# Own moments by SBUF-to-SBUF transfers into free rows: 32 moment slots per tile in place of 36

## What is computed

```python
e = stack([tbl_f[ids[:, f]] for f in range(26)], axis=1)            # (2048, 26, 32)
x1 = einsum('bik,bjk,hij->bhk', e,  e, W1) + b1                      # 128 maps
x2 = einsum('bik,bjk,hij->bhk', x1, e, W2) + b2                      # 128 maps
z = sum(concat([x1, x2], axis=1), axis=-1)                           # (2048, 256)
h = relu(concat([z, dense_ctx], axis=1) @ W_top1 + b_top1)           # 512
h = relu(h @ W_top2 + b_top2)                                        # 256
y = h @ W_top3
```

## Time and profile before

| | us |
|---|---|
| median of 3 runs | 604.69 |
| lowest and highest | 596.48, 609.61 |
| the profiled execution's own time | 604.4 |
| span of its profile | 602.6 |
| mean granted TensorE clock in it | 0.952 of full |

### The profile page before, as it was taken

One profiled execution on the slowest core, in us unless ns is written; L12 is line 12 of the kernel. 1 busy time (PEld: TensorE's weight loads), 2 busy tenths in 40 slices (PEclk: granted clock), 3 DMA queues, 4 the chain that ended last, 5 costly groups with the idle time before them and its releaser, 6 DMA issues.

```text
span 602.6 us, 13628 instructions
## 1 busy us (share of the span) xinstructions
PE 523.6 (87%) x5314; PEld 498.1 (83%) x5314; DVE 454.4 (75%) x1253; ACT 256.9 (43%) x528; POOL 373.7 (62%) x275
## 2 busy tenths in 40 slices
PE   4846986975979989898889898988999789999997
PEld 4524975965979989898889898988989689999987
DVE  6626965949777979697787969595959697996762
ACT  6513762543433535253535262433435253535501
POOL 5774687258735868677676878685858765740100
PEclk9966997996979999998999999998999899999999
DMA  6640022021312141303030213222231303000000
GB/s 194 160 62 8 5 29 36 7 48 22 41 27 33 17 47 16 46 11 47 9 46 12 40 20 36 24 30 29 23 36 16 43 9 44 11 9 1 2 1 2
DMA packets 30925, 19.58 MB, mean 32 GB/s; under 512 B 5171, under 2 KB 30326, under 8 KB 30761
## 3 DMA queue, kind: packets, MB, share of 16 engines
q0 software_dynamic: 8512, 4.38, 10.7%
q1 hardware_dynamic: 22377, 14.73, 9.9%
HBM read 19.08 MB, written 0.01 MB: 32 GB/s over the span
## 4 chain that ended last, share of the span: by engine, by line
PE 83%; issue 7%; ACT 3%; DVE 3%; another core or an unknown queue 2%; DMA 1%; SPq 0%; ACTq 0%; DVEq 0%
PE psum L858 34%; PE psum L878 19%; PE psum L895 11%; PE psum L938 4%; PE psum L916 4%; PE psum L872 3%; PE psum L811 3%; ACT v L699 2%; PE psum L834 1%; PE psum L832 1%; DVE work L624 1%; DMA t_area<-in_L_rec_W 1%; PE psum L804 1%; PE psum L828 1%
## 5 line engine op out<-in xcount | busy, mean ns | idle before, releaser
L377 POOL DMA_INDIRECT emb<-in_tbl,idx x266 | 371.0, 1395 | 162.8 <-issue 76.4
L858 PE MATMUL psum<-diag,work 128*109 128x108 f32 x2048 | 222.2, 266 | 22.2 <-issue 9.1
L858 PEld LDWEIGHTS psum<-diag,work 128*109 128x109 f32 x2048 | 210.6, 180 | 29.2 <-issue 14.7
L728 ACT COPY t_area<-psum 109x432 f32<-109x432 f32 x256 | 130.4, 519 | 193.1 <-PE psum L858 177.4
L624 DVE TENSOR_TENSOR work<-embT 128x32 f32<-128x32 f32 (+12 forms) x416 | 129.2, 387 | 0.0
L895 PE MATMUL psum<-table_parts,onehot 125*128 125x96 bf16 x1350 | 72.7, 213 | 22.5 <-issue 12.4
L895 PEld LDWEIGHTS psum<-table_parts,onehot 125*128 125x128 bf16 x1350 | 66.2, 102 | 27.8 <-issue 22.9
L878 PE MATMUL psum<-t_area,v 128*128 128x128 f32 x608 | 73.0, 277 | 5.3 <-issue 5.3
L878 PEld LDWEIGHTS psum<-t_area,v 128*128 128x128 f32 x608 | 70.5, 193 | 6.4 <-issue 6.3
L712 ACT COPY diag<-embT 32x416 f32<-32x416 f32 x128 | 69.9, 546 | 10.4 <-DVE embT L608 8.8
L454 DVE TENSOR_SCALAR onehot<-ids_left 125x1280 bf16<-125x1280 bf16 (+1 forms) x150 | 57.3, 453 | 0.5
(11 more groups left out here) (103 smaller groups left out, 467.6 us busy)
## 6 DMA issues: line engine op xcount, KB each, us to landing
ids_all<-in_short_ids SPq DMA_DIRECT2D x15, 625.0 KB
emb<-in_tbl,idx POOLq DMA_INDIRECT x266
t_area<-in_L_rec_W SPq DMA_DIRECT2D x1, 1664.0 KB
work<-in_W_top SPq DMA_DIRECT2D x2, 512.0 KB
onehot<-in_tbl SPq DMA_DIRECT2D x5, 156.2 KB
onehot<-in_tbl SPq DMA_DIRECT2D x5, 125.0 KB
t_area<-in_L_rec_W SPq DMA_DIRECT2D x1, 338.0 KB, 3.2
idx<-in_ids SPq DMA_DIRECT2D x4, 52.0 KB, 1.9
```

Source lines behind the costliest of these rows:

```text
L377: eng.indirect_dma_start(emb[n][:, f * K:(f + 1) * K], None, tables[f], bass.IndirectOffsetOnAxis(ap=idx[:, t * F + f:t * F + f + 1], axis=0),
L728: nc.scalar.copy(dst, src).then_inc(t_out, 1)
L858: last = nc.tensor.matmul(dst[:, :, c * TS:(c + 1) * TS], pairs[:, half, g % HALF, c, :], diag[:, g, :, :], start=True, stop=True)
```

## The change

The 13 own slots of a group, as far as their rows are wanted, are cut into six pieces. SyncE copies each from `tsum` to rows 92 and up of the other slots in `tsum` by a DMA, which makes 12 transfers a tile with 284 rows of 512 to 3072 bytes; the other slots then have up to 128 rows for `cin`. Two own slots a group (5 and 6) and the single-field moments ("cross") don't fit; ScalarE copies them: 10 small copies a tile, six of one slot and four of three, three, three and two slots, of 13 to 28 partitions. These `loose` slots are double-buffered. `cin` has 5 + 27 = 32 matmuls. `pack` on VectorE is gone with its buffers and the memsets of `last_packs`.

v is laid out alike: own parts are drained into `staged` and moved by 6 transfers a group. `make_v` has 18 jobs (5 first-layer matmuls where 15 stood), `v_out` 36 copies. VectorE's split of W_top1 and W_top2 moves from behind both halves of `extra` to between them.

```diff
+GAP = CONST + 1
+DEEP = NP - GAP
+PIECES = [(7, 0, DEEP, 0, 0, 6), (11, DEEP, 2 * DEEP, 6, 0, 2), (8, DEEP, tri(11), 8, 0, 3), (0, 0, tri(3), 8, tri(11) - DEEP, 3),
+          (11, 2 * DEEP, CONST, 11, 0, 2), (3, 0, tri(5), 11, CONST - 2 * DEEP, 2)]
+LOOSE = (5, 6)
+CROSS = [(0, 3), (2, 5), (5, 8), (8, 11), (11, 13)]
...
 @block.sync
-            for t in range(2, TILES):
-                eng.wait_ge(left_ready, t - 1)
-                load_ids_all(t)
+            for c in range(2):
+                eng.wait_ge(prep_out, AFTER_V1 if c else AFTER_MOVED + JOBS_W1 + JOBS_OWN)
+                for mu, lo, hi, slot, at, count in PIECES:
+                    dst = V_OTHER + HF * c + slot
+                    eng.dma_start(v[GAP + at:GAP + at + hi - lo, dst:dst + count, :],
+                                  staged[c][lo:hi, mu:mu + count, :]).then_inc(v_moved[c], 16)
+            def pack(t):
+                n = t % 2
+                eng.wait_ge(t_out, UNITS * (t + 1))
+                for mu, lo, hi, slot, at, count in PIECES:
+                    for c in range(2):
+                        src, dst = c * TS + c * HF + mu, c * TS + (1 - c) * HF + slot
+                        eng.dma_start(tsum[GAP + at:GAP + at + hi - lo, n, dst:dst + count, :],
+                                      tsum[lo:hi, n, src:src + count, :]).then_inc(packed[n], 16)
+            for t in range(1, TILES + 1):
+                if t + 1 < TILES:
+                    eng.wait_ge(left_ready, t)
+                    load_ids_all(t + 1)
+                pack(t - 1)
...
 @block.vector
+            for c in range(2):
+                nc.vector.tensor_copy(first_layer[:, c, 0:GAP - c], w1p[:, c, 0:GAP - c])
...
-            nc.vector.memset(packs[:, :, :], 0.0).then_inc(dve_own, 1)
...
+            nc.vector.memset(spare[:, :, :], 0.0).then_inc(loose_zero, 1)
...
-                if not known or t >= 2:
-                    pack(t - 1, 1 - n)
...
 @block.scalar
+            def loose_out(t, n):
+                into = loose[:, n]
+                eng.wait_ge(t_out, UNITS * t + UNITS)
+                for j, (lo, hi) in enumerate(CROSS):
+                    src = tsum[FIELD0:ROWS, n, TS + HF + lo:TS + HF + hi, :]
+                    if j == 0:
+                        for c in range(2):
+                            nc.scalar.copy(tsum[FIELD0:ROWS, n, c * TS + ONE, :], src[:, c, :])
+                    else:
+                        nc.scalar.copy(into[K * (j - 1):K * (j - 1) + HF, 0:hi - lo, :], src)
+                for c in range(2):
+                    for a, mu in enumerate(LOOSE):
+                        at, rows = K * (len(LOOSE) * c + a), tri(mu + 1)
+                        last = nc.scalar.copy(into[at:at + rows, CROSSES, :], tsum[0:rows, n, c * TS + c * HF + mu, :])
+                last.then_inc(loose_ready, 1)
...
                 if u == 0 and isinstance(t, int) and t == 0:
                     eng.wait_ge(extra_ready, 2)
+                    eng.wait_ge(v_moved[0], 16 * len(PIECES))
                 if u == 0 and not (isinstance(t, int) and t < 2):
                     eng.wait_ge(z_full, t - 1)
-                    eng.wait_ge(packs_ready, t - 1)
...
+                if not known or 1 <= t < TILES:
+                    loose_out(t, n)
...
 @block.tensor
-            def cin(t, n):
-                moments, packed = tsum[:, n], last_packs if isinstance(t, int) and t == TILES - 1 else packs
-                eng.wait_ge(packs_ready, t + 1)
+            def cin(t, i, n):
+                eng.wait_ge(packed[n], 16 * PACK_MOVES * (i + 1))
...
+                eng.wait_ge(loose_ready, t + 1)
+                terms = [(V_ONE + c, tsum[:, n, c * TS + ONE, :], ROWS) for c in range(2)]
+                terms += [(V_CROSS + s, loose[:, n, s, :], NP) for s in range(CROSSES)]
...
+                terms = [(V_OTHER + HF * c + nu, tsum[:, n, c * TS + (1 - c) * HF + nu, :], ROWS_OF[nu])
+                         for c in range(2) for nu in range(HF)] + [(V_LOOSE, loose[:, n, CROSSES, :], NP)]
```

More of the change, by code:

```diff
@@ L282, in build @@
         w2T_jobs = [range(m, min(m + 4, F)) for m in range(0, F, 4)]
[L283 to L287, removed]
+        v_jobs = [([("first", 0, s, NP) for s in range(4)], [(0, 4, 0, NP, v[:, 0:4, :])]),
+                  ([("first", 0, 4, NP)], [(0, 1, 0, NP, v[:, 4:5, :])])]
@@ L288, in build, with other_jobs @@
         JOBS_W1 = len(v_jobs)
-        for c in range(2):
+        def other_jobs(c):
+            jobs = []
             for lo in range(0, HF, 4):
                 hi = min(lo + 4, HF)
-                at = (32 * 2 * c, V_P28 + lo) if lo < N28 else (32 * (2 * c + 1), V_P28 + NU_LAST)
-                v_jobs.append(([("other", c, nu, CONST + 1) for nu in range(lo, hi)],
-                               [(0, hi - lo, 0, LOW, LOW * c, V_OTHER + lo), (0, hi - lo, LOW, CONST + 1, *at)]))
+                slot = V_OTHER + HF * c + lo
+                jobs.append(([("other", c, nu, GAP) for nu in range(lo, hi)], [(0, hi - lo, 0, GAP, v[:, slot:slot + hi - lo, :])]))
+            return jobs
@@ L295, in build, with own_jobs @@
+        def own_jobs(c):
+            jobs = []
             for lo in range(0, HF, 4):
+                mus = range(lo, min(lo + 4, HF))
                 moves = []
-                for mu in range(lo, min(lo + 4, HF)):
+                for mu in mus:
                     rows = tri(mu + 1)
[L299 to L304, removed]
@@ L305, in build @@
-                v_jobs.append(([("own", c, mu, tri(mu + 1)) for mu in range(lo, min(lo + 4, HF))], moves))
+                    if mu in LOOSE:
+                        at = K * (len(LOOSE) * c + LOOSE.index(mu))
+                        moves.append((mu - lo, 1, 0, rows, v[at:at + rows, V_LOOSE:V_LOOSE + 1, :]))
+                    else:
+                        moves.append((mu - lo, 1, 0, rows, staged[c][0:rows, mu:mu + 1, :]))
+                jobs.append(([("own", c, mu, tri(mu + 1)) for mu in mus], moves))
@@ L824, in make_v @@
                         dst = prep_bank(n)[0:rows, a * H:(a + 1) * H]
-                        if what == "one":
-                            last = nc.tensor.matmul(dst, w1p[:, c, 0:rows], ident[:, :], start=True, stop=True)
-                        elif what == "cross":
-                            last = nc.tensor.matmul(dst, w1s[c][:, HF + third, 0:rows], ident[:, :], start=True, stop=True)
+                        if what == "first":
+                            last = nc.tensor.matmul(dst, first_layer[:, third, :], ident[:, :], start=True, stop=True)
                         else:
@@ L964, in _ @@
                 short_rows(1, part)
-            cin(0, 0)
+            cin(0, 0, 0)
             for t in range(1, 4):
```

167 lines of the change are left out of this document (69 added, 98 removed).

## The result

| | before | after |
|---|---|---|
| median, us | 602.77 (4 runs) | 648.66 (4 runs) |
| lowest and highest | 596.48, 609.61 | 645.38, 657.79 |
| profiled execution, span | 602.6 | 646.5 |
| mean granted TensorE clock | 0.952 | 0.897 |

What follows compares the result with a forecast made beforehand. TensorE was taken as the bound, by its number of instructions and its standstill. From 604.4 us, 14.3 for `cin` and 4.5 for the preparation gave 585.6, taken as 585.5; range 555 to 603.

Steps and rivals of the forecast that it cites:

- `cin` loses 14.3 us: TensorE's `cin`: four matmuls of 36 fewer in each of 16 tiles, all on the path; -14.3 us, bounds -14.3 and -10.
- VectorE's packing, 0 us; below zero at best: Packing, 8.5 us a tile, leaves VectorE; TensorE never waited for it, so 0, or -35 if it causes the pauses.
- and the change leaves those alone: Claim that TensorE's pauses share a dense run of gathers, which the change doesn't touch; 35 us of standstill stay.
- the rival that pauses go with the packing: In steps 4 to 12, TensorE's 35 us of pauses go in part or whole: 551 to 568 us; chance 0.25.
- The transfers are hidden: The 12 transfers a tile, 5 us of issues and 1.9 of landing, lie beside a 30 us step: 0 us.
- the gain is eaten: Rival: the transfers' rows feed TensorE's pauses, +12 us, and the preparation gives nothing or loses 2: 593 to 603; chance 0.20.
- The preparation, -4.5: Before the loop, `cin(0)` starts at 101.6 instead of 106.05, held by its transfers: -4.5 us, bounds -12 and +2.
- ScalarE's copies: Ten small copies a tile between `fill_diag` and `z_move`, 3.3 us, fit ScalarE's idle time: 0, bounds 0 and +1 a tile.
- SyncE as the bound: Rival: SyncE's ids load, hold and 12 issues set the step from 1.1 us an issue; 626 at 1.4; over 603, chance 0.10.
- The slower outcome: Whole kernel over 617 us, chance 0.08; priced through SyncE's chain of ids load, hold and 12 issues a tile.

Runs made afterwards that it cites:

- e15: Changed kernel without the gathers of tiles 2 to 15, on a chip without pauses: 519.67 us, 0.983 of the kernel before.
- e16: Kernel before without the gathers of tiles 2 to 15, on a chip without pauses: 520.94 us, 0.986 of the kernel before.
- e10: Changed kernel without the gathers of tiles 2 to 15, on a chip with pauses: 534.38 us, where the complete changed kernel took 651.68.
- e11: Kernel before with VectorE's packing copies of tiles 2 to 15 reduced to two of one element: 644.24 us, where the kernel before took 623.79.
- e8: Changed kernel with dummy VectorE copies of the old packing's shapes at its old place: 629.50 us, where the changed kernel took 650.32.
- sets 2 and 3: Two of the five sets of follow-up runs, both on chips with pauses; the kernel before took 622.41 and 623.79 us there.
- e5: The changed kernel as it is, run again on a chip with pauses: 650.32 us, where the kernel before took 622.41.
- e6: The kernel before once more, for its profile on a chip with pauses: 308.9 us from tile 3 to tile 12; its set's median was 622.41 us.
- e7: Changed kernel without the 12 transfers of tiles 2 to 15, on a chip with pauses: 637.34 us, 1.020 of the kernel before.
- e9: The changed kernel as it is, on another chip with pauses: 651.68 us, where the kernel before took 623.79.
- e12: Changed kernel with its first group of one-hot matmuls moved from unit 3 to unit 8: 655.44 us, where the changed kernel took 651.68.
- e18: Changed kernel with tile 0's transfers ahead of tile 2's ids load and two memsets behind each of five gathers a tile: 553.48 us, 1.047 of before.
- e4: Changed kernel without the gathers of tiles 2 to 15, on a chip without pauses: 518.43 us, 0.971 of the kernel before.
- e14: Kernel before with two GpSimd memsets behind each gather of tiles 2 to 15: 657.54 us, 1.244 of the kernel before.

## Why the prediction was wrong

- *`cin` loses 14.3 us*: right in size, where no gather stands in the way. 0.90 a step in e15 against e16, and 6.03 us for 54 instructions.
- *VectorE's packing, 0 us; below zero at best*: this failed. It had a use that no dependency shows: by the counts above it held up the gathers. The step of the prediction that failed is the sentence that the pauses share a dense run of gathers, "and the change leaves those alone". The first half was right (e10). The second was put in doubt by a row in hand: a gather took 1.47 us beside the packing and 0.94 after it. I read this as VectorE hindering GpSimd, and so as a harm that goes; it was a brake that goes. The bounds, 0 and -35, did not hold the other sign. e11 measures it at +20 us in 624, of the 28 that the change cost there, and e8's median agrees (21). Added up for sets 2 and 3, packing +20, transfers +13, `cin` -14 and tile 0 +2 (`cin(0)`'s second half at 116.4 in e5, 114.1 in e6) make 21 of the 28. The 46 of the first comparison is not accounted for beyond that.
- The Trainium skill, page "SBUF — State Buffer", section "SBUF: two separate sides", was cited for the rival that pauses go with the packing. Its rule, that VectorE's fp32 copies and GpSimd exclude each other on a shared port pair, agrees with the gathers' 1.17 to 1.36 us beside the brake for 0.94. What was made of it had the wrong sign. The same section says that engines' ports and the DMA side don't contend and that TensorE waits on nobody's port; so it does not explain the pauses.
- *The transfers are hidden*: 9.1 us a tile of issues for the 5 taken (0.76 each, inside the 0.29 to 0.94), landing 1.99 for 1.9; their rows are of 1024 to 3072 bytes, not from 512 on. No `cin` of the loop waits for them. They are not free all the same: 13 us in e7. Which part is their traffic beside the gathers and which the later ids load was not tried apart. The rival "the gain is eaten" had +12 for this.
- *The preparation, -4.5*: +10.3 in this comparison, and the second term that failed. The path of the transfers was read rightly. They were held behind the ids load, issued at 78.36, and were out at 99.7, so `cin(0)` could have begun near the forecast's 101.6. It began at 115.2, since `short_rows(1)` took 26 us for 5.96 under the run of gathers. Why it was not held up before, with gathers beside it too, is open; e5 and e9 repeat the slow start, and in e8, with the brake, 89 of its 90 matmuls pass in 3.94 us. And where there are no pauses, the same hold costs some 10 us instead of giving 4.5 (e15 against e16), for there the kernel before reaches `cin(0)` at 79.6 (e16). The hidden assumption was that 106.05 is what this kernel needs.
- *ScalarE's copies*: 3.7 us for 3.3; they and `fill_diag` end at 395.3, when `cin` has ended 0.6 us before. Not tried by themselves.
- *SyncE as the bound*: VectorE has no wait for an ids load in the profiles of the changed kernel (the first, e5, e9) and of e12; the price per issue stayed at 0.76 to 0.80 us in the loop, under the 1.1 (tile 0's 12, behind the ids load, took 16.16 us, 1.35 each). The slower outcome came by another mechanism than the one that had been priced for it.

Open: why TensorE and ScalarE pause in a run of gathers, and why on some chips alone. The Trainium skill, page "Runtime: NRT & Kernel Launch", section "Instruction fetch mechanics", says that each sequencer fetches its instructions through a DMA queue of its own; gathers that delay this fetch would fit pauses that wait for nothing shown. The trace speaks against it in the loop. From 290 to 570 us of the changed kernel TensorE has 39 us of "issue" in 64 pauses, most of them in the first row below, and of the 17,269 DMA packets of that stretch four are of an instruction queue, the second row:

```profile
PE psum L918 <- issue: 32.7, 56, 1.7
```

```profile
q14 instruction: 4, 0.03, 0.0%
```

Whether it is GpSimd's work on the gathers or their packets that does it was not tried apart. Whether spacing helps with VectorE untouched is open too; e18 was meant for it and fell on a chip without pauses.

## What to carry to other kernels

Before work is taken off an engine that isn't the bound, ask which other engine it slows, and whether that is a harm or a brake: the row that shows an operation longer beside it speaks for both signs, and the bounds must hold both. Where "issue" takes a share of the chain, find what runs in each pause and what will run there after the change; and before a transfer is put ahead of a load in a queue, look when the load is wanted: here the wait only moved by a step.

## What the runs showed of the hardware

- The same kernel took 532 to 536 us on three chips and 622 to 624 on two others, and 603 in the first comparison. On the second kind TensorE pauses, mostly for 0.3 to 2 us at a time, and ScalarE too, while GpSimd's gathers run closely; the gathers cost 117 us there (e9, e10), where the kernel before and the changed one without gathers differ by 14 to 16 on the first kind (e4, e15).
- The clock falls with the pauses: 0.50 granted from 97 to 113 us, 0.897 on average for 0.952. TensorE is busy for 532.5 us where it was for 523.6, with 148 instructions fewer.
- Small GpSimd instructions are dear where GpSimd has no room: two memsets of 0.2 us each behind every gather took the kernel before from 536 to 658 us (e14).
- An ids load of 640,000 bytes held the issue behind it on SyncE for 7.0 us in the changed kernel and 8.0 in e15, where such an issue takes 0.7 otherwise.
